# Attention by query tile, single scores in half-height TensorE tiles, and a per-chunk query path in a decoder layer with Mamba-2, cross-attention and routed linear layers

## What is computed

```python
x = x + mamba_block(layernorm(x))          # D_INNER 512, state 128, 8 heads of 64, conv of 4 taps, sequential scan
q = heads(layernorm(x)); k, v = heads(ctx) # 16 heads of 16
w = softmax(where(mask == 0, -inf, q @ k.T / 4 + adj))
x = x + (w @ v) @ Wo.T + bo
x = x + take(expert_of_position, layernorm(x) @ W_experts + b)   # one of 8 experts for each of 512 positions
```

## Time and profile before

| | |
|---|---|
| median of 3 runs | 1372.91 us (1369.1 to 1374.38) |
| the profiled execution | 1374.59 us |
| its span | 1372.8 us |
| first stretch, to the first score | 186.0 us |
| eight batches of 64 units, first score to last score | 1079.2 us |
| from the last score to the end | 107.6 us |

### The profile page before, as it was taken

One profiled execution on the slowest core, in us unless ns is written; L12 is line 12 of the kernel. 1 busy time (PEld: TensorE's weight loads), 2 busy tenths in 40 slices (PEclk: granted clock), 3 DMA queues, 4 the chain that ended last, 5 costly groups with the idle time before them and its releaser, 6 DMA issues.

```text
span 1372.8 us, 21799 instructions
## 1 busy us (share of the span) xinstructions
PE 1166.6 (85%) x7020; PEld 768.3 (56%) x7020; DVE 993.5 (72%) x2574; ACT 774.3 (56%) x1380; POOL 579.1 (42%) x533
## 2 busy tenths in 40 slices
PE   0667778998999899999999999999999998877387
PEld 0354545664766576656665666566665665644244
DVE  1764595879777887778787878687868777666386
ACT  0212245666666666656666666666666666677232
POOL 0634573435444454246434633373427331100265
PEclk9867889999999999999999999999999999999799
DMA  6011041313331243114311431143113221311511
GB/s 197 0 62 31 1 129 25 62 32 93 108 62 32 81 120 62 32 47 140 65 38 52 131 70 32 60 129 74 32 43 97 65 54 39 99 47 31 199 55 72
DMA packets 63088, 96.00 MB, mean 70 GB/s; under 512 B 15649, under 2 KB 26145, under 8 KB 61697
## 3 DMA queue, kind: packets, MB, share of 16 engines
q1 hardware_dynamic: 53200, 74.61, 18.1%
q0 software_dynamic: 6240, 17.57, 5.4%
q10 hardware_dynamic: 3536, 2.43, 0.7%
HBM read 71.49 MB, written 27.26 MB: 72 GB/s over the span
## 4 chain that ended last, share of the span: by engine, by line
PE 35%; DVE 20%; POOL 16%; issue 12%; ACT 7%; DMA 1%; DVEq 0%; POOLq 0%; ACTq 0%
PE pm L421 17%; POOL xc L1258 6%; DVE T L1166 5%; PE pt L576 5%; PE po L590 5%; POOL ygT L1255 4%; PE ps L421 3%; ACT PT L783 2%; ACT T L793 2%; PE ps L660 2%; DVE PT L1173 2%; POOL xc L1250 1%; DVE yg L1090 1%; ACT th L743 1%; POOL xdt L1289 1%
## 5 line engine op out<-in xcount | busy, mean ns | idle before, releaser
L793 ACT ACTIVATE T<-T,nmx 128x512 f32<-128x512 f32 x512 | 368.8, 723 | 261.9 <-DVE nmx L1166 261.2
L1166 DVE CUSTOM_DVE_ANT_0 T<-ps,am 128x512 f32<-128x512 f32 x512 | 348.0, 685 | 199.0 <-PE ps L421 197.8
L576 PE MATMUL pt<-ident,T 128*128 128x128 f32 x2048 | 314.7, 277 | 49.8 <-ACT PT L783 47.0
L576 PEld LDWEIGHTS pt<-ident,T 128*128 128x128 f32 x2048 | 250.3, 142 | 149.4 <-ACT T L793 77.7
L421 PE MATMUL ps<-k_st,q_st 128*128 128x512 f32 x512 | 299.7, 586 | 10.9 <-DVE nmx L1166 10.8
L783 ACT COPY PT<-pt 128x512 f32<-128x512 f32 x352 | 201.1, 572 | 60.3 <-PE po L590 59.9
L1258 POOL TENSOR_TENSOR xc<-xc,ygT 128x512 f32<-128x512 f32 x96 | 129.4, 1348 | 14.2
L421 PEld LDWEIGHTS ps<-k_st,q_st 128*128 128x128 f32 x512 | 98.5, 192 | 57.4 <-issue 36.1
L590 PE MATMUL po<-PT,va 128*32 128x512 f32 x1024 | 117.8, 601 | 0.8 <-ACT PT L783 0.8
L1173 DVE COPY PT<-pt 128x512 f32<-128x512 f32 x160 | 109.7, 686 | 8.9 <-PE pt L576 8.7
L1317 POOL TENSOR_TENSOR rr<-se,nhalf 128x1 f32<-128x1 f32 x32 | 17.8, 557 | 226.4 <-DVE se L1096 226.4
(11 more groups left out here) (207 smaller groups left out, 1928.4 us busy)
## 6 DMA issues: line engine op xcount, KB each, us to landing
qk_d<-kp SPq DMA_DIRECT2D x64, 256.0 KB, 2.5
q_st<-qk_d SPq DMA_DIRECT2D x256, 64.0 KB, 2.2
k_st<-qk_d SPq DMA_DIRECT2D x256, 64.0 KB, 2.2
am<-in_mask SPq DMA_DIRECT2D x8, 1024.0 KB, 6.1
am<-in_adj POOLq DMA_DIRECT2D x8, 1024.0 KB, 10.5
x_in<-in_x SPq DMA_DIRECT2D x8, 512.0 KB, 4.6
ctx_in<-in_ctxT SPq DMA_DIRECT2D x8, 512.0 KB, 3.8
x_d<-x SPq DMA_DIRECT2D x32, 128.0 KB, 2.0
```

The costliest lines, as they stand in the source:

```text
L576: ins = pe.transpose(pt[u % 2][:, kt * P:(kt + 1) * P], T[:, u % RING, kt * P:(kt + 1) * P], ident[:, :])
L793: act.activation(T[:, u % RING, :], T[:, u % RING, :], ACT.Exp, bias=nmx[:, u % RING:u % RING + 1], scale=-1.0).then_inc(sems["probs"], 1)
L1166: dve.tensor_tensor_reduce(T[:, u % RING, :], ps[u % 2][:, :], ams[a % 2][:, qt, :], -1.0, 3e38, ALU.add, ALU.min, nmx[:, u % RING:u % RIN ...
```

## The change

- Units go by query tile: 16 units are the 16 heads of one query tile. `pv` comes after every 4 units (16 times a batch, not 4), for one query tile: the same 32 instructions, with 128 columns each. PT shrinks to two buffers of four units. The sums of 16 heads fill po, and copy, turn and division come once for each query tile, as often as before. `ot` and `op` come after each query tile.
- A score takes 64 rows: heads lie alternately on rows 0 to 63 and 64 to 127 of q_st and k_st, and the matmul has a tile position of (0, 0) or (64, 0). Still one instruction for each unit, two ps banks.
- Keys are stored for all 16 heads at once (loads kin, one for each group of 4 heads, 8 DMAs), queries by query tile (qin, 8 DMAs). As many DMAs of 64 KB as before.
- The query path (`q1`, `q2`, `qsplit`) is done for each chunk, on 128 rows: 8 fp32 matmuls of 128 columns for a chunk, where there were 4 of 512 columns for two tiles each in a batch.
- `seg` is two fp32r matmuls over a high and a low part of the decay mask, not one fp32 matmul (two instructions either way); POOL makes both parts (L1281 twice).
- The table is new, in 20 ticks a slot, with one table for batch 0 and one for the others. The later chunks of a batch stand beside its own first units. In batch 0, on TensorE, what is behind the first score is: z, inter, intra, out projection of chunk 3, and the queries of chunks 2 and 3 (and q2 of chunk 1).
- The waits for loads are split by what is needed (ident, x, weights). Convolution of batch 0: two tiles on POOL, four on VectorE. `route` moves to batch 6, in three steps, through the pm banks. Memsets of V move to POOL; those of q_st and k_st go.
- x1, On and other buffers are smaller or shared, and xqT, qf, sq, dmask have buffers of their own.

```diff
-UG = HG * C
-UNITS = G * UG
+UNITS = C * AH
-PV = UG + LAG
+PV = HG + LAG
+OUT = AH + LAG
...
     def unit(u):
-            w = u % UG
-            return u // UG, w % C, w // C
+            return u // AH, u % AH
...
     def score(a, u):
-                    g, qt, hh = unit(u)
-                    n, hs = u // (HS * C), u // C % HS
+                    qt, h = unit(u)
...
                     pe.wait_ge(sems["row_max"], at("row_max", a, u - 1))
-                    mm(ps[u % 2][:, :], q_st[:, n % 2, hs, qt * P:(qt + 1) * P], k_st[:, n % 2, hs, :], True, True).then_inc(sems["score"], 1)
+                    half = slice(h % 2 * P // 2, (h % 2 + 1) * P // 2)
+                    pe.matmul(ps[u % 2][:, :], q_st[half, qt % 2, h // 2, :], k_st[half, h // 2, :], start=True, stop=True,
+                              tile_position=(h % 2 * P // 2, 0)).then_inc(sems["score"], 1)
...
     def pv(a, n):
+                    g = n % G
                     for kt in range(C):
                         for hh in range(HG):
-                            ins = pe.matmul(po[VW * hh:VW * (hh + 1), :], vas[a % 2][:, kt, g * HG + hh, :], PT[:, hh, kt, :],
+                            ins = pe.matmul(po[VW * hh:VW * (hh + 1), g * P:(g + 1) * P], vas[a % 2][:, kt, g * HG + hh, :], PT[:, n % 2, hh, kt, :],
                                             start=(kt == 0), stop=(kt == C - 1), tile_position=(0, VW * hh), skip_group_check=True)
...
     if k == "seg":
-                        mm(bank(("seg", j, c), b)[:, :], stril[:, :], dmask[:, 4 * j:4 * j + 4, :].rearrange("p h i -> p (h i)"), True, True)
+                        for hl in range(2):
+                            ins = mm(bank(("seg", j, c), b)[:, :], stril[:, :], dmask[:, hl, 4 * j:4 * j + 4, :].rearrange("p h i -> p (h i)"), hl == 0, hl == 1)
...
     if k == "q2":
-                        for kt in range(KE):
-                            ins = mm(bank(("q", ct), b)[:, :], wq[:, kt, ct * P:(ct + 1) * P], xqT[:, kt, :], kt == 0, kt == KE - 1)
+                        for ct in range(KE):
+                            for kt in range(KE):
+                                ins = mm(bank(("q", c), b)[:, ct * P:(ct + 1) * P], wq[:, kt, ct * P:(ct + 1) * P], xqT[:, kt, :], kt == 0, kt == KE - 1)
...
+                    if k == "kin":
+                        g = stg[1]
+                        sp.wait_ge(sems["k_out"], at("k_out", b, 16 * 4))
+                        sp.wait_ge(sems["score"], at("score", b, -AH + HG * (g + 1)))
+                        k_in(b, g)
+                    if k == "qin":
+                        c = stg[1]
+                        sp.wait_ge(sems["q_out"], at("q_out", b, 16 * 4 * (c + 1)))
+                        sp.wait_ge(sems["score"], at("score", b, AH * (c - 1)))
+                        q_in(b, c)
...
     if k == "dmask":
+                        for hl in range(2):
+                            pool.tensor_tensor(dmask[:, hl, :, :], triu[:, :] ..., dA2[:, hl, c, :] ..., ALU.mult).then_inc(sems["decay_mask"], 1)
```

More of the change, by code:

```diff
@@ L299, in build @@
[L299 removed]
+        sp_loads = [((ident[:, :], t["ident"]), ident_in), (matrix(wxbc, "wxbc"), w_in),
+                    ((cw[:, :, :], t["conv_w"].rearrange("(k p) j -> p k j", p=P)), consts), (column(cb, "conv_b"), consts)]
+        act_loads = [(column(lnw, "ln_w"), ln_in), (column(lnb, "ln_b"), ln_in), (matrix(wdt, "wdt"), w_in), (row(alog[:, :], "A_log"), consts)] + [
+            (row(dtb[:, c, :], "dt_bias"), consts) for c in range(C)] + [((triu[:, :], t["triu"]), consts), (matrix(wk, "wk"), kv_in), (matrix(wv, "wv"), kv_in)]
@@ L546, in m @@
+                    if k == "r3":
+                        pe.wait_ge(step["f_tables"], 1)
+                        pe.wait_ge(read(stg, b), free_at(stg, b))
+                        for c in range(C):
+                            ins = mm(bank(stg, b)[:, 0:BLOCKS], tmp[:, LEFT + c * P:LEFT + (c + 1) * P], tmp[:, RIGHT + c * BLOCKS:RIGHT + (c + 1) * BLOCKS], c == 0, c == C - 1)
+                        ins.then_inc(full(stg, b), 1)
                     if k == "ot":
@@ new lines, in route @@
+                n_at = S // SEG
+                dve.wait_ge(full(stg, b), full_at(stg, b))
+                product = bank(stg, b)
+                if stg[0] == "r1":
+                    sc, key = view(ST, C, NT), view(ST + 32, C, NT)
+                    best, top = view(ST + 64, C), view(ST + 68, C)
+                    scores = product[:, 0:C * NT].rearrange("p (c t) -> p c t", t=NT)
+                    then(dve.tensor_reduce(best, scores, AX.X, ALU.max))
+                    dve.tensor_tensor(sc, scores, over(best, [P, C, NT], 2), ALU.is_equal).then_inc(read(stg, b), 1)
+                    dve.wait_ge(read(stg, b), read_at(stg, b))
+                    then(dve.tensor_tensor(key, sc, over(rcol["first"], [P, C, NT], 1), ALU.mult))
+                    then(dve.tensor_reduce(top, key, AX.X, ALU.max))
+                    dve.tensor_tensor(oh, key, over(top, [P, C, NT], 2), ALU.is_equal).then_inc(step["f_onehot"], 1)
@@ new lines, in route @@
+                if stg[0] == "r3":
+                    held, empty = view(ST + 580, BLOCKS), view(ST + 590, BLOCKS)
+                    then(dve.tensor_scalar(empty, product[:, 0:BLOCKS], 0.0, 1e6, ALU.is_equal, ALU.mult))
+                    dve.scalar_tensor_tensor(held, product[:, 0:BLOCKS], -1.0, empty, ALU.add, ALU.add).then_inc(read(stg, b), 1)
+                    dve.wait_ge(read(stg, b), read_at(stg, b))
+                    dve.tensor_copy(row_of[:, :], held).then_inc(step["f_rows"], 1)
```

773 lines of the change are left out of this document (415 added, 358 removed), and 12 rows, old and new, of tables (FIRST, STAGES, TAIL).

## The result

The changed kernel takes 1414.62 us, the median of 4 runs (1412.95 to 1416.38), beside 1372.68 (1369.1 to 1374.38) for the kernel before on the same chip: a ratio of 1.0309, 95% interval 1.0284 to 1.0334. It is 3.1% slower. The forecast was 1465, 6.7% slower: the sign is right, the size more than twice too large (92 us against 42).

The account below looks back on a forecast made before the run. TensorE bounds the middle batches, the chain from engine to engine the last. Before the first score 116, work behind it 1174, idle 73, end 102: 1465 us, against 1373, 6.7% slower; own range 1415 to 1515, with rivals 1292 to 1515.

Parts of the forecast that it names:

- The step at the scores: On TensorE, each score's change from full height to half and back costs 0.37 us, 23.7 us a batch; chance 0.64.
- The product with V: On TensorE, 16 visits a batch, not 4, with rounds of 0.12 us: 21.0 us where it was 15.1, +5.9.
- The first stretch: Time before the first score: 116 us (100 to 140), where it was 186.0.
- (-10, -25, +5): Before the first score: -10 us for small loads, -25 for set-up, route and convolution, +5 for TensorE's longer k and v list.
- Idle time: TensorE idle over the eight batches: 73 us, from 136.1; last batch 31 to 10, the others 15.3 to 9.
- The end: Behind the last score: a shorter product with V and one query tile of Wo, 107.6 - 5.6 = 102 us.
- POOL's second mask: On POOL, for seg: 4 x 1.9 = 7.6 us a batch, hidden, but seg waits if POOL is late.
- SP's late queries: On SP, a batch's first query tile load stands behind keys of head group 2: 1 us of stall a batch.
- The first (no step, 1314 us): Rival at the scores: half-height scores cost no step, 1314 us, 4.3% faster; chance 0.27.
- The threshold: At the scores: the change gains only if the step costs over 0.18 us less than put, so under 0.19.
- The second rival: No step at the scores, but rounds of short products with V at 0.22 us: 102 us more, 1416; chance 0.05.
- The third (idle time stays at 136): Rival on the new order: scores wait for per-chunk queries on SP and POOL, TensorE idle stays 136: 1528 us; chance 0.04.

Follow-up runs that it names:

- run 1: Changed kernel with each score a matmul over all 128 rows, without tile position, the two heads of a pair not separated: 1310.53 us, ratio 0.9551.
- run 2: Kernel before with each score on rows 0 to 63 alone, always the same tile, in the old order: 1453.52 us, ratio 1.0605.
- run 5: Changed kernel with full-height scores, heads kept apart by zeros in the other head's half, V tiles in steps of 18 elements: 1309.66 us, ratio 0.9547.
- run 4: Changed kernel with seg as before, one fp32 matmul over one POOL mask instead of two fp32r ones: 1425.08 us, ratio 1.0375.
- run 3: Kernel before with the product with V cut into 128-column instructions, 128 in a visit, still four visits a batch: 1374.45 us in one execution.
- run 6: Changed kernel with scores issued two at a time in opposite halves, a ring of five score rows and packed V tiles: 1387.22 us, ratio 1.0115.

## Why the prediction was right in sign and wrong in size

**The step at the scores** was the heart of it, and it is right: 0.37 us forecast, 0.34 measured, in both orders (runs 1, 2 and 5). The unit is 1.01 us, not 1.04: 0.03 x 512 = 15 us less. That a change of rows costs like one of columns was argued from the V visits and is now measured: 0.34 against 0.33.

**The product with V is the step that failed**, in "I take 0.12: 16 x (0.96 + 0.35) = 21.0 us". The sum charges every visit with a whole change of shape and back, beside a whole one for every score. But a score follows at once in 76 of the 128 visits, and there leaving the 32-column tiles and entering the half rows is one change. Run 5, with full height on both sides of a visit, has this stretch (V, score, transposes, next product):

```profile
613.22 1.08 PE L708 MATMUL po<-PT,va_all 128*32 128x128 f32 x32
614.23 0.50 PE L504 MATMUL ps<-k_st,q_st 128*128 128x512 f32 x1
614.57 0.60 PE L691 MATMUL pt<-ident,T 128*128 128x128 f32 x4
615.00 1.88 PE L504 MATMUL pm<-wz,xnT 128*128 128x512 f32 x4
```

It takes 615.00 - 613.22 = 1.78 us, and the same stretch of the changed kernel 715.69 - 713.76 = 1.93. A half-height score right behind the product with V costs 0.15 more than a full-height one, where it costs 0.34 behind a transpose or a product of z. So 0.19 us were counted twice in 76 visits: 14 us. The two smaller parts are the round, 0.109 and not 0.12 us (8 x 0.011 x 128 = 11 us), and the step of a visit, 0.33 and not 0.35 (3 us). With full height on both sides a visit adds 1.20 us: 202 ns to its start, 808 to its last instruction, and 738 from there to the third instruction of an out projection, where it is 543 behind a transpose. In front of a score it adds 1.01. Together that is 17.4 us a batch, not 21.0, and 28 us of the miss of 50.

**The first stretch** was put at 116 us and took 107.0; 9 us. TensorE's list was quicker than I had it, and the load of the queries ended last:

```profile
99.81 0.38 PE L624 MATMUL pm<-ident,xnr 128*128 128x128 f32 x2
107.04 0.80 PE L679 MATMUL ps<-k_st,q_st 64*128 64x512 f32 x2 [6.85 <-DMA q_st<-q_d]
```

The list before the first score is done at about 100 us, 11 to 16 earlier than my 111 to 116, and then 6.85 us of wait for a DMA stand there that my sum did not have. The two errors partly cancel. Which of the terms (-10, -25, +5) was off was not tried.

**Idle time** was 73 us in the sum. With the measured terms the work behind the first score is 8 x (64.6 + 17.4 + 1.7) + 7 x 63.5 + 15 = 1129, which leaves 1206 - 1129 = 77 of 1206 us, 4 more. It is a remainder, and takes the errors of the 63.5 and the 15 with it. It is not all idle: the granted clock, for which the prediction has no term, was 0.97 over these 1206 us, which is up to 35 us, and 0.98 over before's 1079, up to 17. At 565.6 us, for example, it falls to 1.2 GHz, when TensorE has just waited 2.57 us for a row maximum. That the remainder came out near the forecast is in part luck. **The end** was put at 102 and took 101.4.

**The sum**: 15 + 28 + 9 + 1 - 4 = 49 us, the miss of 50 but for rounding. As the forecast's own difference was 92 us, these small terms, nearly all of one sign, are more than half of it. The prediction gives its case with the step a range of 1415 to 1515, and the measured 1414.6 lies just below its lower end; the bounds that it names (idle time 30 to 136, first stretch 100 to 140) give 1406 to 1552.

**Hidden work.** POOL's second mask (2.09 us each, had 1.90) is hidden in the eight batches: no wait of TensorE there is put down to POOL. In the first stretch it is not. TensorE idles 10.35 us before its first seg product at 46.01, and POOL makes both masks from 41.46 to 45.90 just before, so the second one stands for some 2 us there. The query path is 4 fp32 matmuls for a chunk, 8 instructions, as the prediction counts it, and not 8 matmuls. SP's late queries cost a middle batch 0.5 us, against the 1 us I put, by TensorE's waits:

```profile
PE ps L679 <- DVE nmx L1254: 3.4, 2, 2.6
PE pt L687 <- ACT PT L880: 1.7, 2, 0.8
PE ps L679 <- DMA q_st<-q_d: 0.5, 1, 0.5
```

**The rivals.** The first (no step, 1314 us) was priced right: runs 1 and 5, which are that case, gave 1310.5 and 1309.7. Its sum put 14 us of idle time in each batch rather than 9; the theories of the experiments, which let idle time take up or give back too little, 1283 in run 1, 1485 in run 2 and 1437 in run 4, missed by 12 to 32 us. The threshold that I worked out from the forecast, a gain below 0.19 us a score, was too low, since the sum was 50 us too high. The second rival (no step, 0.22 a round) has the number that came closest, 1416 against 1414.6, by luck: both its conditions are false, by runs 1 and 3. The third (idle time stays at 136) falls with the first batch: 138.9 us, TensorE busy 137.2.

## What to carry to other kernels

Count the changes of TensorE's tile shape in the order in which instructions are issued, not the visits: two tile shapes next to each other share one. In this kernel a half-height tile saved storage, not time, when it was issued alone between full-height products; zeros in the other half of the rows, for 8 KB of each partition, were worth 104 us. And turn saved or added TensorE work into time through the idle time of the stretch: here 40 to 65% of it showed in the kernel's time.

## What the runs showed of the hardware that I had not expected

- Two matmuls in opposite row halves run side by side: starts 3 ns apart, the pair in the 0.43 us of one (run 6).
- The step has a tail: the second transpose behind a half-height score starts 165 ns after the first, not 109; the later ones are on time.
- Rounds of four 128-column fp32 products in 32-column tiles take 0.109 us, within 2% of the quarter of a 512-column round (run 3), with new weights for every instruction. Whole-array products do not get shorter below 128 columns here: 0.111 us with 64 columns, 0.109 for a transpose.
- A change of shape that joins two tile shapes is paid once: a half-height score right behind 32-column tiles costs 0.15 us more than a full-height one, not 0.34 (run 5 and the changed kernel).
